# Expert rows transposed on the way in: DMA for TensorE and ScalarE, and one batch's normalization moved to VectorE

## The chip, the cores and the metric

The kernel runs on one core of a Trainium2 chip. The metric is the time of one execution on the device in microseconds. Seen in the profile are the core's engines: TensorE (matrix multiply, PE in the rows; PEld is its weight load), VectorE (DVE), ScalarE (ACT), GpSimd (POOL) and SyncE (SP), which only issues transfers. Each works through its own list of instructions in order; semaphores tie the lists together, and 16 DMA engines serve the transfers of all.

## What is computed

One gated block: cross-attention over a context of 77 tokens, added to x, then a layer of routed experts, added to that. x is 4 x 1024 x 256, float32. Cut to what matters:

```
x = x + tanh(g_xattn) * attention(layernorm(x), ctx)       # 4 batches x 1024 tokens, 77 keys each
h = layernorm(x)
gate = softmax(h @ gate_w + gate_b)                         # 8 experts
top_val, top_idx = top_k(gate, 2)
hidden = relu(h @ w1[e] + b1[e])                            # 256 -> 1024
expert_out[e] = hidden @ w2[e] + b2[e]                      # 1024 -> 256
x = x + tanh(g_ffn) * sum_k top_val[k] * expert_out[top_idx[k]]
```

Each token goes to two of eight experts. The kernel computes only the chosen ones.

## The kernel before

**Precision.** An expert's matmuls are done in float16 with each operand split into a high and a low half, so that three products stand for one of float32. The weights are split at the start: ScalarE writes the high part (hi_part, line 736), VectorE the low part (lo_part, line 958), for eight experts and two weights each. A token's normalized row is stored in the same way: high_rows on ScalarE (line 787) and low_rows on VectorE (line 1218) write 256 high and 256 low halves into xext, beside 8 gates and the token's number. That is a row of 265 words (XW), 1060 bytes.

**Routing.** For each batch of 1024 tokens VectorE picks the experts and a place for each token in a table in DRAM, xs, with 4096 rows for each expert. GpSimd writes the rows there with 16 indirect scatters a batch (scatter_rows, line 579). The table is then worked through in tiles of 128 rows that belong to one expert, S = 71 tiles. Of those, the tiles that are full after batch r may be read as soon as batch r is scattered; which table row a tile starts at, and which expert it is, lies in row_tab and exp_tab, made while the loop runs.

**The expert loop.** In iteration s of 71 each engine does its part, in an order written out by hand:
- SP, load_rows(s) (lines 487 to 501): reads the tile's first row from row_tab and loads 128 rows of xs into xg[s % 4], one transfer of 132.5 KB. Before it reuses the buffer it waits until tile s - 4 was transposed (line 497), its gates taken (line 498) and its indices copied (line 499).
- TensorE, turn_rows(s + 2) (line 1711): four 128x128 transposes of the row's high and low halves, into bank 5; then hidden(s + 1), 32 matmuls in eight column blocks (lines 1730 to 1734), and output(s), 24 matmuls (lines 1752 to 1754).
- ScalarE, rows_T(s + 2) (line 856): copies bank 5 to xTh[s % 2]; then h_bias (line 866), eight activations that add the bias to one half of the sums, h_hi (line 875), the high half of relu, and y_scale (line 882).
- VectorE: gate(s + 2) (line 1400), h_sum (line 1407), h_low (line 1415), y_sum (line 1422).
- GpSimd: index(s + 2) (line 652) and scatter(s) (line 660), an indirect transfer that adds 128 result rows to the output in DRAM. Scatter s waits until scatter s - 1 has landed.

**What runs beside it.** Attention for batches 0 and 1 and the splitting of the weights come before the loop. The attention of batches 2 and 3 runs inside it, one tile of 128 tokens for each iteration (attention_steps: iterations 2 to 16 and 18 to 32). A tile of attention goes through turn, rows_copy (line 767), scores (line 1593), score_in (line 1173) with the row maxima (line 1176), softmax_exp (line 772), turn_prob, attend and residual (line 1192). The parts attention_start, attention_mid and attention_end say where each engine does this between its expert work.

**Second normalization.** After attention a batch's 8 tiles of 128 tokens are normalized: rows_norm_2, on VectorE for batch 0 (line 1213) and on GpSimd for batches 1, 2 and 3 (line 612). It may start when the batch's x was stored to the output (s_outd). On GpSimd, batch 1 is done before the expert loop. ScalarE converts batch 1's rows (high_rows(1)) after its first two rows_T and ahead of the first h_bias.

**Buffers.** xg, xTh and the hidden buffers lie in pool0, in the space of the raw weights of two experts. The first transfers into it wait until VectorE is done with the first of these (s_lo1), hidden(0) until it is done with two (s_lo1 at 2), h_bias(0) for s_lo at 7 and VectorE's first h_sum for s_lo at 8.

Of the kernel before, what the change touches and what calls it, by code (L numbers as in the profile page):

```python
# [5 lines left out]
def gated_attention_and_routed_experts(  # L6
# [10 lines left out]
    ALU = mybir.AluOpType  # L17
# [35 lines left out]

    xs = nc.dram_tensor("xs", (E * N + P, XW), F32, kind="Internal").ap()

    with ExitStack() as ctx:
# [26 lines left out]

        xg = [carve(XW) for _ in range(U)]
        xTh = [carve(2 * ND * P, F16) for _ in range(2)]
        hb = carve(NH * P)
# [281 lines left out]
        g_ix = sem("g_ix")  # L368
        g_T = sem("g_T")
        g_xT = sem("g_xT")  # L370
        g_mm1 = sem("g_mm1")
# [9 lines left out]
        s_raw = [sem(f"s_raw{k}") for k in range(4)]  # L381
        g_xg = [sem(f"g_xg{u}") for u in range(U)]

        def tile_tokens(ap, b):
# [22 lines left out]
        ranked = bank[7][:, 2 * P:2 * P + 2 * E].rearrange("p (j e) -> p j e", j=2)  # L407
        turned_x = bank[5][:, 0:ND * P].bitcast(F16)
        summed = bank[4][:, 0:D]
# [20 lines left out]
        def _(sp):  # L430
# [58 lines left out]
            def load_rows(s):  # L489
                r = round_of(s)  # L490
                sp.wait_ge(s_tab, 3 * (r + 1))
                sp.wait_ge(s_scat, min(r + 1, B) * KO * T * 16)
                if r == B:
                    sp.wait_ge(s_pads, 2 * E * 16)
                    sp.wait_ge(s_zst, 16)
                if s >= U:
                    sp.wait_ge(g_T, s - U + 1)
                    sp.wait_ge(g_q, s - U + 1)
                    sp.wait_ge(g_ix, s - U + 1)
                row = sp.value_load(row_tab[0:1, s:s + 1], min_val=0, max_val=E * N)  # L500
                sp.dma_start(xg[s % U], xs[ds(row, P), :]).then_inc(g_xg[s % U], 16)

# [19 lines left out]
        def _(pool):  # L522
# [121 lines left out]
            root(3)  # L644
            rows_norm_2(1, 0, T)
            token_ids(1)

            def index(s):
                pool.wait_ge(g_xg[s % U], (s // U + 1) * 16)
                if s >= U:  # L650
                    pool.wait_ge(g_out, (s - U + 1) * 16)
                g.tensor_copy(idx[s % U][:], xg[s % U][:, TC:XW].bitcast(I32)).then_inc(g_ix, 1)

# [42 lines left out]
        def _(act):  # L696
# [134 lines left out]
            gate_exp(1)  # L831
            hi_part(7, 0)
            hi_part(6, 1)
            hi_part(7, 1)
# [10 lines left out]
            def attention_mid(s):  # L845
                for b, j in attention_steps(s):
                    for i in tile_at(j - 2):
                        rows_copy(b, i)
                    if j in (13, 14):
                        high_rows(b, 4 * (j - 13), 4 * (j - 12))  # L850

            def rows_T(s):
                act.wait_ge(g_T, s + 1)
                if s >= 2:
                    act.wait_ge(g_mm1, NHB * (s - 1))
                a.copy(xTh[s % 2], turned_x).then_inc(g_xT, 1)

# [25 lines left out]

            rows_T(0)
            rows_T(1)
            high_rows(1, 0, T)
            act.wait_ge(s_lo, E - 1)
# [3 lines left out]
            for s in range(S):  # L891
                attention_start(s)
                if s + 2 < S:
                    rows_T(s + 2)
                if s + 1 < S:
                    h_bias(s + 1)
                    h_hi(s + 1)
                attention_mid(s)
                y_scale(s)
# [3 lines left out]
        def _(dve):  # L903
# [426 lines left out]
            scales(3)  # L1330
            choose_2(1)
            lo_part(6, 0)
            gates(1)
# [62 lines left out]
            def gate(s, e):  # L1396
                if s >= U:
                    dve.wait_ge(g_y2, s - U + 1)
                dve.wait_ge(g_xg[s % U], (s // U + 1) * 16)
                v.tensor_tensor(q[s % U][:], xg[s % U][:, ds(e + GC, 1)].to_broadcast([P, 2]), inv[:, ds(2 * e, 2)], ALU.mult).then_inc(g_q, 1)  # L1400

# [45 lines left out]
        def _(pe):  # L1447
# [254 lines left out]

            def turn_rows(s):
                pe.wait_ge(g_xg[s % U], (s // U + 1) * 16)
                if s:
                    pe.wait_ge(g_xT, s)
                o = turned_x
                x16 = xg[s % U][:, 0:D].bitcast(F16)
                for c in range(ND):
                    for k in range(2):  # L1710
                        mm = t.transpose(o[:, (2 * c + k) * P:(2 * c + k + 1) * P],  # L1711
                                         x16[:, k * D + c * P:k * D + (c + 1) * P], ident16[:])
                mm.then_inc(g_T, 1)

            def hidden(s):
                pe.wait_ge(g_xT, s + 1)
                xt = xTh[s % 2]
                for c in range(NH):
# [43 lines left out]
            load_adr(0, 2 * NH)  # L1762
            turn_rows(0)
            turn_rows(1)
            pe.wait_ge(s_lo1, EB)
# [3 lines left out]
            for s in range(S):  # L1769
                if s == 1:  # L1770
                    pe.wait_ge(s_lo, E)
                if s + 2 < S:
                    turn_rows(s + 2)
                if s + 1 < S:
                    hidden(s + 1)
                else:
                    load_adr(s, 4 * NH)
                attention_mid(s)
                output(s)
                attention_end(s)  # L1780
# [28 lines left out]
```

## Time and profile before

| | us |
|---|---|
| median of 3 runs | 639.74 (639.56 to 641.3) |
| the profiled execution | 637.47 |
| its span in the profile | 635.7 |
| TensorE busy, matmuls (4723) | 521.8 (82%) |
| TensorE busy, weight loads (4724) | 432.8 (68%) |
| ScalarE busy (1061 instructions) | 416.6 (66%) |
| VectorE busy (1149) | 402.7 (63%) |
| GpSimd busy (296) | 286.0 (45%) |
| SP's queue (q1), share of the DMA engines | 18.7% |
| GpSimd's queue (q0) | 16.8% |

Busy is the time in which an engine has an instruction at work; matmuls overlap, and their ends are modelled. The profiled execution lies 2.3 us under the median, and 1.8 us of it are outside the span. The mean granted clock of TensorE is 0.875 of full speed. The span falls into three parts: up to about 144 us the weights, the attention of two batches and their routing; then the expert loop with attention inside it, to about 445 us; then the expert loop alone.

### The profile page before, as it was taken

The page shows a single profiled execution, that of the slowest core. Times are in us where ns is not written, and L with a number is a line of the kernel's source. Part 1 is how long each engine was busy: PE and PEld are TensorE (multiplying, and loading weights), DVE is VectorE, ACT ScalarE, POOL GpSimd, SP SyncE. Part 2 cuts the span into 40 slices and gives each one's busy share as a digit, 9 for nine tenths or more (in the row PEclk, how much of TensorE's full clock was granted, in tenths as well). Part 3 has the DMA queues.
Part 4 walks back from the last instruction along what each step waited for, and adds up shares of the span by engine and source line. Part 5 has one row for each costly group of instructions (what it writes and reads, how often), then busy time and mean ns, then how long its engine had stood idle before and what let it go on. Part 6 is the DMA issues. An engine that isn't in the chain of part 4 may idle for free.

```text
span 635.7 us, 15679 instructions
## 1 busy us (share of the span) xinstructions
PE 521.8 (82%) x4723; PEld 432.8 (68%) x4724; DVE 402.7 (63%) x1149; ACT 416.6 (66%) x1061; POOL 286.0 (45%) x296
## 2 busy tenths in 40 slices
PE   6958317506888999987799998879999999999991
PEld 3637216205567887765588887657999999999991
DVE  3268799487485667773467677745755566666650
ACT  2567874555456676664476675746888888888880
POOL 3110228574673323766532337666476632233331
PEclk8775555556899999998899999979999999999997
DMA  6919405723533223233232233233333333333221
GB/s 171 331 52 379 165 0 195 274 75 110 161 69 69 36 43 83 54 66 95 74 52 36 35 71 74 56 91 88 61 73 57 53 53 52 53 52 52 35 28 17
DMA packets 47633, 57.07 MB, mean 90 GB/s; under 512 B 6855, under 2 KB 43197, under 8 KB 47423
## 3 DMA queue, kind: packets, MB, share of 16 engines
q1 hardware_dynamic: 32223, 36.60, 18.7%
q0 software_dynamic: 14064, 18.55, 16.8%
q10 hardware_dynamic: 1264, 0.93, 0.5%
q8 instruction: 40, 0.66, 0.5%
q14 instruction: 42, 0.34, 0.2%
HBM read 33.19 MB, written 24.49 MB: 91 GB/s over the span
## 4 chain that ended last, share of the span: by engine, by line
PE 48%; DVE 16%; issue 10%; ACT 9%; DMA 6%; POOL 4%; SPq 2%; another core or an unknown queue 1%; ACTq 1%; DVEq 1%; POOLq 0%
PE hid L1730 8%; PE hid L1734 8%; PE bank L1752 6%; PE bank L1753 6%; PE bank L1754 6%; ACT pool L866 4%; PE hid L1731 4%; PE hid L1733 4%; POOL xb L612 3%; DMA out_dram<-pool,idx 3%; DVE pool L1407 2%; DMA xb<-in_x_dram 2%; DVE w1l L958 2%; PE bank L1711 2%; DVE w2l L958 2%
## 5 line engine op out<-in xcount | busy, mean ns | idle before, releaser
L660 POOL DMA_INDIRECT out_dram<-pool,idx x71 | 114.8, 1617 | 224.7 <-DVE pool L1422 190.4
L866 ACT ACTIVATE pool<-hid,b1s 128x128 f32<-128x128 f32 x568 | 167.7, 374 | 42.8 <-remote 24.1
L1730 PE MATMUL hid<-pool,w1h 128*128 128x256 f16 x568 | 159.1, 280 | 14.2 <-DVE pool L1407 7.5
L1752 PE MATMUL bank<-w2h,pool 128*128 x568 | 155.8, 274 | 9.5 <-issue 8.9
L1734 PE MATMUL hid<-pool,w1h 128*128 128x256 f16 x568 | 159.1, 280 | 1.9 <-issue 1.9
L1407 DVE TENSOR_TENSOR pool<-hid,pool 128x512 f32<-128x512 f32 x142 | 97.0, 690 | 96.3 <-ACT pool L866 96.2
L1753 PE MATMUL bank<-w2l,pool 128*128 x568 | 155.9, 274 | 2.1 <-issue 1.8
L1754 PE MATMUL bank<-w2h,pool 128*128 x568 | 155.9, 275 | 0.5 <-issue 0.5
L1731 PE MATMUL hid<-pool,w1l 128*128 128x128 f16 x568 | 127.2, 224 | 0.3 <-issue 0.3
L1733 PE MATMUL hid<-pool,w1l 128*128 128x128 f16 x568 | 127.1, 224 | 0.4 <-issue 0.3
L875 ACT ACTIVATE pool<-pool 128x512 f16<-128x512 f32 x142 | 90.1, 637 | 32.1 <-DVE pool L1407 31.6
L1415 DVE SCALAR_TENSOR_TENSOR pool<-pool 128x512 f16<-128x512 f32 x142 | 95.2, 686 | 5.4
L579 POOL DMA_INDIRECT xs<-xext,dest x64 | 72.8, 1137 | 31.0 <-issue 22.2
L1730 PEld LDWEIGHTS hid<-pool,w1h 128*128 x568 | 56.7, 100 | 24.0 <-issue 22.0
L1752 PEld LDWEIGHTS bank<-w2h,pool 128*128 128x128 f16 x568 | 55.9, 98 | 17.0 <-issue 9.9
L1753 PEld LDWEIGHTS bank<-w2l,pool 128*128 128x128 f16 x568 | 55.9, 98 | 12.0 <-issue 5.2
L1733 PEld LDWEIGHTS hid<-pool,w1l 128*128 x568 | 57.1, 100 | 8.7 <-issue 0.5
L1731 PEld LDWEIGHTS hid<-pool,w1l 128*128 x568 | 56.8, 100 | 7.5 <-issue 1.5
L1754 PEld LDWEIGHTS bank<-w2h,pool 128*128 128x128 f16 x568 | 55.9, 98 | 8.5 <-issue 1.7
L1734 PEld LDWEIGHTS hid<-pool,w1h 128*128 x568 | 56.9, 100 | 2.4 <-issue 2.4
L1422 DVE SCALAR_TENSOR_TENSOR pool<-pool,q 128x256 f32<-128x256 f32 x71 | 34.3, 484 | 32.7 <-ACT pool L882 26.1
L882 ACT ACTIVATE pool<-bank,q 128x256 f32<-128x256 f32 x71 | 33.5, 472 | 30.4 <-PE bank L1754 21.9
(257 smaller groups left out, 764.4 us busy)
## 6 DMA issues: line engine op xcount, KB each, us to landing
pool<-in_L_ffn_w_dram SPq DMA_DIRECT2D x12, 1024.0 KB
pool<-xs SPq DMA_DIRECT2D x71, 132.5 KB
xb<-in_x_dram SPq DMA_DIRECT2D x4, 1024.0 KB
out_dram<-xb SPq DMA_DIRECT2D x4, 1024.0 KB, 5.0
out_dram<-pool,idx POOLq DMA_INDIRECT x71
w1h<-in_L_ffn_w_dram SPq DMA_DIRECT2D x1, 1024.0 KB, 5.1
w1l<-in_L_ffn_w_dram SPq DMA_DIRECT2D x1, 1024.0 KB, 7.6
w2h<-in_L_ffn_w_dram SPq DMA_DIRECT2D x1, 1024.0 KB, 9.7
```

The costliest lines, as they stand in the source:

```text
L660: g.indirect_dma_start(out=out_rows, out_offset=bass.IndirectOffsetOnAxis(ap=idx[s % U][:, 0:1], axis=0), in_=y2[s % 3], in_offset=None, c ...
L866: a.activation(hb[:, c * P:(c + 1) * P], bank[c // 2][:, (2 * (c % 2) + 1) * P:2 * (c % 2 + 1) * P], ACT.Identity, bias=b1s[:, ds(e * NH + ...
L875: a.activation(hh[s % 2][:, half], hb[:, half], ACT.Relu).then_inc(g_hh, 1)
L1407: v.tensor_tensor(part, main, part, ALU.add).then_inc(g_hb, 1)
L1415: v.scalar_tensor_tensor(hl[s % 2][:, half], hb[:, half], 0.0, hh[s % 2][:, half], ALU.max, ALU.subtract).then_inc(g_hl, 1)
L1730: t.matmul(o, wh, xhl, start=True, stop=False)
L1731: t.matmul(o[:, 0:P], wl, xh, start=False, stop=False)
L1733: t.matmul(o[:, 0:P], wl, xh, start=False, stop=False)
L1734: mm = t.matmul(o, wh, xhl, start=False, stop=True)
L1752: t.matmul(o, hh[s % 2][:, hs], wh, start=c == 0, stop=False)
L1753: t.matmul(o, hh[s % 2][:, hs], wl, start=False, stop=False)
L1754: mm = t.matmul(o, hl[s % 2][:, hs], wh, start=False, stop=c == NH - 1)
```

## The change

An expert tile's rows no longer come as they lie. Of each tile SP issues four transfers with transpose=True, one for each 128x128 block of float16 (two column halves, high and low), from xs seen as float16 into xTh[s % 4], and then one transfer of the rest of the row, 9 words (8 gates and the token's number), into a smaller xg[s % 4]. TensorE's turn_rows, ScalarE's rows_T, bank 5's view and their semaphores are gone. There are now four xTh buffers instead of two, each with a semaphore g_xT[u], which hidden(s) waits for at 64 for each use. SP reuses the buffers of a slot when hidden(s - 4) is done (g_mm1), instead of when its rows were transposed; the waits for gates and indices stay.

The normalization of batch 1 after attention goes from GpSimd to VectorE, behind choose_2(1) and ahead of lo_part(6, 0). ScalarE's high_rows(1) moves from behind rows_T(1) to between hi_part(7, 0) and hi_part(6, 1). Batches 2 and 3 stay on GpSimd.

```
     xs = nc.dram_tensor("xs", (E * N + P, XW), F32, kind="Internal").ap()
+    xs16 = xs.bitcast(F16)
...
-        xg = [carve(XW) for _ in range(U)]
-        xTh = [carve(2 * ND * P, F16) for _ in range(2)]
+        xTh = [carve(2 * ND * P, F16) for _ in range(U)]
+        xg = [carve(XW - D) for _ in range(U)]
         hb = carve(NH * P)
...
         g_ix = sem("g_ix")
-        g_T = sem("g_T")
-        g_xT = sem("g_xT")
         g_mm1 = sem("g_mm1")
...
         g_xg = [sem(f"g_xg{u}") for u in range(U)]
+        g_xT = [sem(f"g_xT{u}") for u in range(U)]
...
         ranked = bank[7][:, 2 * P:2 * P + 2 * E].rearrange("p (j e) -> p j e", j=2)
-        turned_x = bank[5][:, 0:ND * P].bitcast(F16)
         summed = bank[4][:, 0:D]
...
                 if s >= U:
-                    sp.wait_ge(g_T, s - U + 1)
+                    sp.wait_ge(g_mm1, NHB * (s - U + 1))
                     sp.wait_ge(g_q, s - U + 1)
...
                 row = sp.value_load(row_tab[0:1, s:s + 1], min_val=0, max_val=E * N)
-                sp.dma_start(xg[s % U], xs[ds(row, P), :]).then_inc(g_xg[s % U], 16)
+                for c in range(ND):
+                    for k in range(2):
+                        sp.dma_start(xTh[s % U][:, (2 * c + k) * P:(2 * c + k + 1) * P],
+                                     xs16[ds(row, P), k * D + c * P:k * D + (c + 1) * P], transpose=True).then_inc(g_xT[s % U], 16)
+                sp.dma_start(xg[s % U], xs[ds(row, P), D:XW]).then_inc(g_xg[s % U], 16)
...
             root(3)
-            rows_norm_2(1, 0, T)
             token_ids(1)
...
                     pool.wait_ge(g_out, (s - U + 1) * 16)
-                g.tensor_copy(idx[s % U][:], xg[s % U][:, TC:XW].bitcast(I32)).then_inc(g_ix, 1)
+                g.tensor_copy(idx[s % U][:], xg[s % U][:, TC - D:XW - D].bitcast(I32)).then_inc(g_ix, 1)
...
             hi_part(7, 0)
+            high_rows(1, 0, T)
             hi_part(6, 1)
...
                         high_rows(b, 4 * (j - 13), 4 * (j - 12))
-
-            def rows_T(s):
-                act.wait_ge(g_T, s + 1)
-                if s >= 2:
-                    act.wait_ge(g_mm1, NHB * (s - 1))
-                a.copy(xTh[s % 2], turned_x).then_inc(g_xT, 1)
...
-            rows_T(0)
-            rows_T(1)
-            high_rows(1, 0, T)
             act.wait_ge(s_lo, E - 1)
...
                 attention_start(s)
-                if s + 2 < S:
-                    rows_T(s + 2)
                 if s + 1 < S:
...
             choose_2(1)
+            rows_norm_2(1, 0, T)
             lo_part(6, 0)
...
                 dve.wait_ge(g_xg[s % U], (s // U + 1) * 16)
-                v.tensor_tensor(q[s % U][:], xg[s % U][:, ds(e + GC, 1)].to_broadcast([P, 2]), inv[:, ds(2 * e, 2)], ALU.mult).then_inc(g_q, 1)
+                v.tensor_tensor(q[s % U][:], xg[s % U][:, ds(e + GC - D, 1)].to_broadcast([P, 2]), inv[:, ds(2 * e, 2)], ALU.mult).then_inc(g_q, 1)
...
-            def turn_rows(s):
-                pe.wait_ge(g_xg[s % U], (s // U + 1) * 16)
-                if s:
-                    pe.wait_ge(g_xT, s)
-                o = turned_x
-                x16 = xg[s % U][:, 0:D].bitcast(F16)
-                for c in range(ND):
-                    for k in range(2):
-                        mm = t.transpose(o[:, (2 * c + k) * P:(2 * c + k + 1) * P],
-                                         x16[:, k * D + c * P:k * D + (c + 1) * P], ident16[:])
-                mm.then_inc(g_T, 1)
-
             def hidden(s):
-                pe.wait_ge(g_xT, s + 1)
-                xt = xTh[s % 2]
+                pe.wait_ge(g_xT[s % U], (s // U + 1) * ND * 2 * 16)
+                xt = xTh[s % U]
                 for c in range(NH):
...
             load_adr(0, 2 * NH)
-            turn_rows(0)
-            turn_rows(1)
             pe.wait_ge(s_lo1, EB)
...
                     pe.wait_ge(s_lo, E)
-                if s + 2 < S:
-                    turn_rows(s + 2)
                 if s + 1 < S:
```

## Rows read from the trace of the kernel before

**Rows 1.** Stretches: busy us of PE, PEld, DVE, ACT, POOL; clock, DMA share.

```profile
322.00:376.00 54.00, 53.30 (x532) 46.79 (x530) 36.20 (x97) 38.14 (x119) 14.16 (x16) 1.00 0.25 37
...
505.00:600.00 95.00, 95.00 (x1041) 86.72 (x1040) 57.47 (x105) 79.64 (x209) 29.99 (x34) 1.00 0.31 50
```

**Rows 2.** Timeline, GpSimd: start us, us, engine, line; [idle before, releaser].

```profile
206.70 1.56 POOL L660 DMA_INDIRECT out_dram<-pool,idx  x1 [5.36 <-DVE pool L1422]
...
249.10 1.56 POOL L660 DMA_INDIRECT out_dram<-pool,idx  x1 [5.27 <-DVE pool L1422]
...
278.48 2.90 POOL L660 DMA_INDIRECT out_dram<-pool,idx  x1 [4.25 <-DVE pool L1422]
...
315.85 1.59 POOL L660 DMA_INDIRECT out_dram<-pool,idx  x1 [4.92 <-issue]
...
446.10 1.59 POOL L660 DMA_INDIRECT out_dram<-pool,idx  x1 [3.37 <-DVE pool L1422]
...
616.59 1.57 POOL L660 DMA_INDIRECT out_dram<-pool,idx  x1 [3.73 <-DVE pool L1422]
```

**Rows 3.** Chain that ended last, late stretch: start us, us, what.

```profile
603.71 0.22 PE bank L1711 x4
```

**Rows 4.** Timeline, ScalarE, one iteration with attention.

```profile
207.20 0.36 ACT L772 ACTIVATE pr<-pr,nms 128x77 f32<-128x77 f32 x1 [1.91 <-DVE nms L1176]
...
207.56 0.56 ACT L856 COPY pool<-bank 128x512 f16<-128x512 f16 x1
208.02 2.18 ACT L866 ACTIVATE pool<-hid,b1s 128x128 f32<-128x128 f32 x8
```

**Rows 5.** Timeline, TensorE's weight loads, the end of that iteration.

```profile
211.90 0.52 PEld L1593 LDWEIGHTS bank<-KQ,xT 128*128 128x128 f32 x4 [0.36 <-ACT xT L767]
```

**Rows 6.** Timeline at the loop's start: GpSimd, ScalarE, VectorE.

```profile
133.52 16.73 POOL L612 TENSOR_SCALAR xb<-xb,mv,rs 128x256 f32<-128x256 f32 x8 [0.69 <-DMA out_dram<-xb]
...
150.33 1.90 ACT L787 CAST xext<-xb 128x2048 f16<-128x2048 f32 x1 [4.60 <-POOL xb L612]
...
144.63 4.61 DVE L958 SCALAR_TENSOR_TENSOR w2l<-pool,scl,w2h 128x2048 f16<-128x2048 f32 x2
...
153.31 0.69 DVE L1407 TENSOR_TENSOR pool<-hid,pool 128x512 f32<-128x512 f32 x1 [1.96 <-ACT pool L866]
```

**Rows 7.** Groups by line: busy us, mean ns | idle before.

```profile
L1213 DVE TENSOR_SCALAR xb<-xb,mv,rs 128x256 f32<-128x256 f32 x8 | 2.7, 408 | 0.0
```

**Rows 8.** SP: timeline of first loads; line 501 in ns, min/median/max.

```profile
140.92 3.90 SPq L501 DMA_DIRECT2D pool<-xs  x4
...
L501 SPq DMA_DIRECT2D pool<-xs x71: 16/338/369, 140.9 to 591.7; - x71
```

**Rows 9.** Timeline, GpSimd, one indirect scatter of 128 rows.

```profile
119.48 0.96 POOL L579 DMA_INDIRECT xs<-xext,dest  x1 [0.30 <-issue]
```

**Rows 10.** Timeline, TensorE, the first transposes.

```profile
143.09 0.61 PE L1711 MATMUL bank<-ident,pool 128*128 128x128 f16 x4 [5.25 <-DMA pool<-xs]
```

**Rows 11.** SP's waits over the span: us in all, times, longest.

```profile
SPq L498 <- DVE q L1400: 152.7, 43, 11.4
```

**Rows 12.** DMA queues, 505 to 600 us: packets, MB, share of engines.

```profile
q0 software_dynamic: 2448, 2.23, 20.2%
q1 hardware_dynamic: 2436, 2.29, 9.5%
```

**Rows 13.** Timeline, GpSimd, four late scatters.

```profile
572.63 1.57 POOL L660 DMA_INDIRECT out_dram<-pool,idx  x1 [3.73 <-DVE pool L1422]
...
578.21 1.55 POOL L660 DMA_INDIRECT out_dram<-pool,idx  x1 [3.81 <-DMA out_dram<-pool,idx]
...
621.85 1.55 POOL L660 DMA_INDIRECT out_dram<-pool,idx  x1 [3.69 <-DVE pool L1422]
...
626.45 1.55 POOL L660 DMA_INDIRECT out_dram<-pool,idx  x1 [3.05 <-DMA out_dram<-pool,idx]
```

**Rows 14.** Waits from 281 to 316 us: us in all, times, longest.

```profile
ACT pool L866 <- remote: 10.0, 5, 3.7
```

## The prediction

> **What bounds the kernel now.** I began with the page, whose busy times put TensorE first, and then read stretches. From 505 to 600 us TensorE is busy all of the time at a granted clock of 1.00, its 2.4 GHz level, and the next engine, ScalarE, for 79.6 of 95 us; from 322 to 376 us TensorE is busy for 53.3 of 54 us [rows 1]. A busy engine need not set the pace, so the two stretches have to be told apart by their chains. GpSimd issues one accumulating scatter for each expert tile, and the starts of these scatters give the period of a tile [rows 2]. From 446.10 to 616.59 us there are 31 periods of 5.50 us. From 206.70 to 249.10 us, where the attention of the third batch (index 2 in the code) runs inside the expert loop, there are 6 of 7.07 us; the fourth batch repeats this with 6 more of 7.05 us.
>
> In the late stretch the chain of waits is TensorE alone, matmul after matmul without a gap, and the four transposes stand in it with 0.22 us [rows 3]. TensorE's own list of instructions is the bound there, and 0.22 us of 5.50 is what the change takes away.
>
> In the attention stretch the bound is a loop over three engines. ScalarE waits 1.91 us for VectorE's row maxima, runs the exponential, then the copy of the transposed rows (line 856) and the eight bias activations (line 866) without idle time between [rows 4]. VectorE's sums wait for these, ScalarE's line 875 for the sums, the copy of line 767 ends ScalarE's part, and TensorE, held 0.36 us for it [rows 5], scores the next attention tile, from which the maxima come. The row copy takes 0.56 us, but the first bias activation starts 0.46 us after it; those 0.46 us are inside the loop.
>
> **The change, part by part.**
>
> *Transposes and copy removed.* Four transposes and one copy go from each of 71 tiles. In the late stretch that is 31 x 0.22 = 6.8 us. In the 12 regular attention periods the loop loses 0.46 us: 5.5 us. TensorE doesn't stop this: of 7.05 us it has 0.36 idle and sheds at least the 0.22 of its transposes, so it could run at 6.47 against the loop's 6.59; it is then the next to be late. Of the 70 periods, 12 and 31 are now counted and the last two follow the last rows. Of the other 25, 11 lie where GpSimd puts four of a batch's row scatters between two accumulates, or right behind that; four of them, from 278.48 to 315.85, average 9.3 us [rows 2], and TensorE stands there for "issue" and for no row. I credit them nothing. Four are held by GpSimd's own normalization of the third and fourth batch, which stays: nothing. The remaining 10 get 0.3 us each, between 0.22 and 0.46: 3 us. Ends of this term: 0, and 25 x 0.46 = 11.5 us.
>
> *The second batch's normalization (index 1) on VectorE.* On GpSimd it took 16.73 us from 133.52 on; ScalarE waited 4.60 us for it before its conversion at 150.33, the first bias activations came behind that, and VectorE's first sum at 153.31 waited for them [rows 6]. On VectorE eight such rows took 2.7 us in the first batch [rows 7]. Their wait for the store of x1 costs nothing, since GpSimd's began at 133.52 and the place in VectorE's queue, behind choose_2(1), comes after that. Behind them are queued the low weight parts (line 958), the gates and the places, and SP, TensorE and ScalarE wait for the weight parts. The last pair, 4.61 us from 144.63, ends at 149.24 [rows 6], and so at 151.9. VectorE is then the one that is late: first sum at 151.9 for 153.31, a gain of 1.4 us. ScalarE's conversion (1.90 us) moves ahead of its last two weight parts, two engines' work side by side; VectorE, 2.7 us later itself, doesn't wait for them. TensorE's wait before its second tile shortens too, and it may keep the upper clock: I count nothing, at best 2 us.
>
> *Four transposing transfers and a short one.* No row shows a transposing transfer. SP needs 3.90 us for four loads now, of which the last instruction is 0.34: (3.90 - 0.34) / 3 = 1.19 us a load, 0.34 of it the transfer's own [rows 8]. Lower bound for a new tile: each of four more transfers like that instruction, 1.19 + 4 x 0.34 = 2.5 us of SP, and nothing below, since each is one more instruction. Upper bound: each like GpSimd's indirect scatter of 128 rows, 0.96 us with 0.30 of gap [rows 9], 1.19 + 4 x 1.26 = 6.2 us, on SP or in the queues. I take 0.5 us each, 3.2 us in all, near the lower end, because the transfers are issued by SP and with a direct pattern as the 0.34 us one is. That is hidden under a period of 5.28 us. The latency has more cover: a buffer comes free with hidden(s-4) and is read by hidden(s), four periods less a first layer of 2.6 us, so 18.5 us; a load now takes 2.2 us (issued at 140.92, used at 143.09 [rows 8, 10]). SP's last wait for a load is for VectorE's gates now (line 498, 152.7 us in all [rows 11]); the new one on g_mm1 comes about a first layer after it, and behind it stand only later loads and the stores of x1. The short transfer is last, so gates and indices get their data some 2 us later, inside the same cover. At the start there is none: SP is released by a weight part of VectorE, 2.7 us later than now, so it issues from 143.6; with 4 x 0.5 of issue and the rest of the landing hidden(0) starts at 147.3, while ScalarE may not begin its bias before 149.6, when the part that it waits for is done. At 1.26 each it is 150.0, and little of the 1.4 us is left.
>
> The DMA engines: from 505 to 600 us SP's queue takes 9.5% and GpSimd's 20.2% [rows 12], so 0.53 us of a tile for its 128 rows and 1.1 us for the accumulate. 512 pieces of 256 bytes and 128 short ones cost between once and five times the 0.53: 1.6 to 3.8 of 5.28 us with the accumulate.
>
> Of such a transfer only the notes have a price. The Trainium skill, "VectorE: DVE Perf Modes", section "The three transpose paths", gives 1309 ns for a 128x128 bf16 block by DMA and 390 ns on TensorE; this case's transposes take 0.22 us for four in a row, and no run here shows the other. An estimate from that page, if the transfers don't overlap, is 4 x 1.309 + 1.19 = 6.4 us a tile, which would be the first rival below. The Trainium skill, "Advanced Engine Details and Errata", section "X-Bar Transpose (TRN2)", says that such transfers are as fast as regular ones, which would be the forecast.
>
> **Sum.** 6.8 + 5.5 + 3 + 1.4 = 16.7 us. The profiled execution took 637.47 us (span 635.7); less 16.7 that is 620.8. The median of the runs shown stands 2.3 us above it, 639.74, so 623.0 us.
>
> **Rivals.**
>
> *1, slower: the transfers set the pace.* If a tile's five transfers take longer than 5.50 us on SP or in the queue, each late tile waits for its rows, and four buffers only put that off. At the upper bound the price is 31 x (6.2 - 5.50) = 21.7 us; attention's loop of 6.6 us stays the bound there (-5.5 us); the start and the ten other periods give nothing. 639.7 + 16.2 = 656 us. For it: five instructions in one queue instead of one. Against it: a load lands within 2.2 us. It decides from (5.50 - 1.19) / 4 = 1.08 us a transposing transfer on.
>
> *2, a smaller gain: the chain of accumulates.* A scatter waits for the landing of the one before. Undisturbed, the last two start 4.60 us apart [rows 13], which leaves 0.68 us under 5.28. One late scatter was held for its forerunner's landing and started 5.58 us after it, at 578.21 [rows 13]. If the denser queue does that to every tile, the late period is 5.58: 639.7 - 1.4 - 5.5 + 31 x 0.08 = 635 us.
>
> *3, slower: late issue.* From 281 to 316 us ScalarE's line 866 waits five times for something that the profile calls "remote", 10.0 us in all [rows 14], while the DMA queues are full of row scatters; the four periods there are 3.8 us longer than late ones. If the new transfers bring that about in every fourth late tile, it costs 8 x 3.8 = 30 us: 639.7 - 16.7 + 30 = 653 us.
>
> **How the numbers follow.** Forecast 623 us, chance 0.50; its own range is 612 (the other 25 periods at 11.5 us, the clock kept) to 631 (the other periods and the start at nothing, half of attention's gain). Rival 1 has 0.24, rival 2 0.10, rival 3 0.10, and 0.06 is for gains and losses that cancel. About 0.3% is what a measurement of this kernel can tell from no change. Faster by more: the forecast and most of rival 2, 0.58. Within it: 0.08. Slower: 0.34. The range of 611 to 660 holds the forecast and the three rivals at their prices and leaves out only dearer transfers than the upper bound.
>
> **What would show it.** Right: scatter starts 5.28 us apart late and 6.6 us in attention, line 1730 without idle time put down to the transfers into pool, the first sum near 152 us. Wrong: line 1730 waiting for those transfers from 446 us on (rival 1); line 660 waiting for its own landing in each tile (rival 2); more and longer waits for "issue" and "remote" in the late stretch (rival 3). If attention's period stays at 7.05, my reading of its loop is wrong; if the first sum is not before 153.3, VectorE's queue or the first landing was dearer than I took it. One transposing transfer of over 1.08 us in steady work would make the forecast wrong by itself.

## The result: 8% slower, and SP is the bound

| | before | after |
|---|---|---|
| median on the same chip, us | 639.65 (636.74 to 641.3, 4 runs) | 690.8 (687.99 to 697.78, 4 runs) |
| ratio, 95% interval | 1 | 1.0832 (1.0778 to 1.0885) |
| profiled execution, us (span) | 637.47 (635.7) | 691.21 (689.5) |
| mean granted clock | 0.875 | 0.854 |

The forecast was 623 us and the range ended at 660. The sign was wrong, and the mechanism that won is the first rival, at more than its price. The profile's page of the kernel after shows where to look. These are its busy times, the DMA packets and queues, and the shares of the chain that ended last, by engine and by line:

```profile
PE 526.9 (76%) x4439; PEld 420.4 (61%) x4440; DVE 396.8 (58%) x1157; ACT 381.8 (55%) x990; POOL 266.8 (39%) x288
...
DMA packets 93073, 57.08 MB, mean 83 GB/s; under 512 B 61383, under 2 KB 88637, under 8 KB 92863
...
q1 hardware_dynamic: 77663, 36.64, 21.5%
...
SPq 27%; PE 23%; DVE 14%; issue 14%; ACT 9%; DMA 8%; POOL 1%; another core or an unknown queue 1%; ACTq 1%; DVEq 1%; POOLq 0%
SPq L502 20%; PE hid L1711 5%; PE hid L1715 4%; ACT pool L863 3%; DVE pool L1400 3%; PE bank L1733 2%; PE hid L1712 2%; PE bank L1735 2%; PE hid L1714 2%; DMA xb<-in_x_dram 2%; PE bank L1734 2%; DMA out_dram<-pool,idx 2%; SPq L504 2%; DVE w1l L950 2%; SPq L499 2%
```

ScalarE and GpSimd have less to do, as the change says. No computing engine is full, and the queue of SP, which computes nothing, leads the chain with 27%, 20% of it the one line that issues the transposing transfers (502). SP's timeline at the loop's start is the plainest view (start, us, SP's queue, line, operation, count). A group x4 is one tile's four blocks:

```profile
138.15 5.03 SPq L502 DMA_TRANSPOSE pool<-xs  x4
143.40 0.41 SPq L504 DMA_DIRECT2D pool<-xs  x1
144.61 5.77 SPq L502 DMA_TRANSPOSE pool<-xs  x4
...
163.67 0.42 SPq L504 DMA_DIRECT2D pool<-xs  x1
164.14 0.42 SPq L510 DMA_DIRECT2D pool<-in_L_ffn_b_dram  x1
```

Then the line's own durations over the whole run (ns, min/median/max), and who waited for the short transfer (line 504), which is issued after the four:

```profile
L502 SPq DMA_TRANSPOSE pool<-xs x284: 21/1150/2510, 138.2 to 662.9; - x142
...
L504 SPq DMA_DIRECT2D pool<-xs x71: 212/427/1186, 143.4 to 664.2; - x71
...
  DVE q L1393: 81.3, 25
  POOL idx L654: 50.9, 19
```

A transposing transfer holds SP's queue for 1.15 us in the median, where a whole tile's plain load held it for 0.34 [rows 8]. The chain in the late stretch is SP, block after block. Its pieces in order of time are start, us, what:

```profile
599.17 1.14 SPq L502
...
600.44 1.15 SPq L502
...
603.12 0.42 SPq L504
...
604.45 1.14 SPq L502
...
608.26 2.18 SPq L502
...
610.65 2.56 DMA pool<-xs
...
613.44 0.16 DVE q L1393
```

One block starts 1.27 us after the other. Five instructions and their bookkeeping make a cycle of about 6.5 us, from 138.15 to 144.61 and here from 597.93 to 604.45, and now and then a block takes about a microsecond more, as the 2.18. That is above the 5.50 us that TensorE needed before [rows 2, 3]. In the kernel before, SP waited 152.7 us for VectorE's gates [rows 11]. In after no such wait is left, and SP's waits for a free buffer (line 497) come to 24.4 us in 10 times. SP is nearly always at work, and the others wait for it. A stretch that answers to [rows 1], its waits, and its scatter starts [rows 2]:

```profile
505.00:600.00 95.00, 82.86 (x797) 69.10 (x796) 44.59 (x86) 57.67 (x161) 33.00 (x37) 0.96 0.32 42
```

```profile
DVE q L1393 <- DMA pool<-xs: 72.6, 23, 5.1
```

```profile
470.83 1.58 POOL L662 DMA_INDIRECT out_dram<-pool,idx  x1 [4.74 <-DVE pool L1415]
...
529.14 1.56 POOL L662 DMA_INDIRECT out_dram<-pool,idx  x1 [2.86 <-DVE pool L1415]
...
670.99 1.57 POOL L662 DMA_INDIRECT out_dram<-pool,idx  x1 [3.90 <-DVE pool L1415]
```

TensorE was busy for 95.0 of 95 us and is now for 82.86. From 480 to 660 us VectorE's gates (line 1393) wait 72.6 us, 23 times, for rows. The 31 late periods take 200.2 us for 170.5: 6.46 us each, and 6.75 in the last 21, once the four buffers in hand are used up. (6.5 us is a cycle without a long block; about one transposing transfer in twelve takes a microsecond more.) The DMA engines aren't the bound: from 560 to 640 us their share by queue is

```profile
q0 software_dynamic: 1722, 1.57, 17.3%
q1 hardware_dynamic: 9230, 1.60, 13.4%
```

against 20.2% and 9.5% before [rows 12]. What is full is the list of instructions that issues, not what moves the bytes.

**Where the 53.8 us of the span come from**, by scatter starts. The loop's first accumulate starts 13.0 us later (177.95 for 164.99). The next four periods cost 2.2 us, the late stretch 29.7, and the stretches in which GpSimd's row scatters lie between the accumulates 4.1 (291.95 to 353.18 us in after) and 8.2 (423.38 to 470.83). The other periods with attention give back 2.8 and the last two 0.6: 13.0 + 2.2 + 29.7 + 4.1 + 8.2 - 2.8 - 0.6 = 53.8.

The change costs more at the start than these 13.0 us. VectorE finishes the variances of batch 1, which come ahead of anything that was changed, at 125.47 us in after and at 129.61 in before: the profiled execution of after happened to be 4.1 us quicker up to there (granted clock of the first 50 us 0.88 for 0.76). Counted from this mark, the first accumulate comes after 52.5 us instead of 35.4, which is 17.1 us later.

The start has a second cause beside the pace of SP. These are after's rows there, of VectorE and ScalarE (compare [rows 6]), and one wait from 138 to 200 us:

```profile
132.26 2.67 DVE L1205 TENSOR_SCALAR xb<-xb,mv,rs 128x256 f32<-128x256 f32 x8
...
152.49 0.16 DVE L1393 TENSOR_TENSOR q<-pool,inv 128x2 f32 x1 [4.71 <-DMA pool<-xs]
152.56 1.28 DVE L1400 TENSOR_TENSOR pool<-hid,pool 128x512 f32<-128x512 f32 x2
```

```profile
135.01 1.90 ACT L789 CAST xext<-xb 128x2048 f16<-128x2048 f32 x1
```

```profile
DVE xext L1210 <- DMA pool<-in_L_ffn_b_dram: 14.1, 1, 14.1
```

The normalization takes 2.67 us on VectorE and is over before its rows are wanted. VectorE's gate of the second tile, which stands ahead of its first sum, waits 4.71 us for that tile's short transfer, the tenth instruction of SP's list. And the bias of the second layer (line 510) is issued by SP behind four tiles' loads. These were four instructions and are now twenty, so it goes out at 164.14 (149.27 before), VectorE stands 14.1 us for it, and behind VectorE wait GpSimd's row scatters and its first accumulate.

### The profile page after: what moved, and what is told of

Same layout as the page of the kernel before. It is cut to its first block, busy times and chain, and to the rows that moved or that the text cites. A ratio compares the mean times of both kernels' runs of the same rounds, so it can differ in the third digit from the quotient of the medians.

```text
span 689.5 us, 15469 instructions
## 1 busy us (share of the span) xinstructions
PE 526.9 (76%) x4439; PEld 420.4 (61%) x4440; DVE 396.8 (58%) x1157; ACT 381.8 (55%) x990; POOL 266.8 (39%) x288
## 3 DMA queue, kind: packets, MB, share of 16 engines
q1 hardware_dynamic: 77663, 36.64, 21.5%
## 4 chain that ended last, share of the span: by engine, by line
SPq 27%; PE 23%; DVE 14%; issue 14%; ACT 9%; DMA 8%; POOL 1%; another core or an unknown queue 1%; ACTq 1%; DVEq 1%; POOLq 0%
SPq L502 20%; PE hid L1711 5%; PE hid L1715 4%; ACT pool L863 3%; DVE pool L1400 3%; PE bank L1733 2%; PE hid L1712 2%; PE bank L1735 2%; PE hid L1714 2%; DMA xb<-in_x_dram 2%; PE bank L1734 2%; DMA out_dram<-pool,idx 2%; SPq L504 2%; DVE w1l L950 2%; SPq L499 2%
## 5 line engine op out<-in xcount | busy, mean ns | idle before, releaser
L1711 PE MATMUL hid<-pool,w1h 128*128 128x256 f16 x568 | 164.9, 290 | 57.1 <-DVE pool L1400 37.0
L1715 PE MATMUL hid<-pool,w1h 128*128 128x256 f16 x568 | 165.4, 291 | 2.2 <-issue 2.2
L1733 PE MATMUL bank<-w2h,pool 128*128 x568 | 158.0, 278 | 11.1 <-issue 10.2
L1734 PE MATMUL bank<-w2l,pool 128*128 x568 | 157.9, 278 | 5.7 <-issue 5.7
L1735 PE MATMUL bank<-w2h,pool 128*128 x568 | 157.8, 278 | 5.3 <-issue 5.3
L1400 DVE TENSOR_TENSOR pool<-hid,pool 128x512 f32<-128x512 f32 x142 | 94.6, 687 | 86.1 <-ACT pool L863 80.1
L1712 PE MATMUL hid<-pool,w1l 128*128 128x128 f16 x568 | 131.1, 231 | 3.7 <-issue 3.6
L1714 PE MATMUL hid<-pool,w1l 128*128 128x128 f16 x568 | 131.1, 231 | 0.8 <-issue 0.8
L1711 PEld LDWEIGHTS hid<-pool,w1h 128*128 x568 | 58.6, 103 | 79.1 <-issue 76.8
L582 POOL DMA_INDIRECT xs<-xext,dest x64 | 70.6, 1103 | 35.4 <-issue 22.2
L1393 DVE TENSOR_TENSOR q<-pool,inv 128x2 f32 x71 | 12.0, 170 | 105.7 <-DMA pool<-xs 81.3
L1733 PEld LDWEIGHTS bank<-w2h,pool 128*128 128x128 f16 x568 | 56.7, 100 | 24.6 <-issue 16.2
L1712 PEld LDWEIGHTS hid<-pool,w1l 128*128 x568 | 58.7, 103 | 13.8 <-issue 3.5
L1714 PEld LDWEIGHTS hid<-pool,w1l 128*128 x568 | 59.1, 104 | 12.2 <-issue 1.7
L1715 PEld LDWEIGHTS hid<-pool,w1h 128*128 x568 | 59.2, 104 | 2.2 <-issue 2.2
L654 POOL COPY idx<-pool 128x1 int32<-128x1 int32 x71 | 38.3, 540 | 50.9 <-DMA pool<-xs 50.9
```

What stands on the lines that cost most here:

```text
L1400: v.tensor_tensor(part, main, part, ALU.add).then_inc(g_hb, 1)
L1711: t.matmul(o, wh, xhl, start=True, stop=False)
L1712: t.matmul(o[:, 0:P], wl, xh, start=False, stop=False)
L1714: t.matmul(o[:, 0:P], wl, xh, start=False, stop=False)
L1715: mm = t.matmul(o, wh, xhl, start=False, stop=True)
L1733: t.matmul(o, hh[s % 2][:, hs], wh, start=c == 0, stop=False)
```

## The experiments

The kernels ran on chips that differ in their absolute time (the kernel before took 611 to 640 us), so each is given as a ratio to the kernel before on the same chip. A ratio still moves a little from chip to chip: the same kernel gave 1.0832 and 1.0868 (after), and 0.9824 and 0.9737 (e9 and e14 below). So ratios of different chips that lie within 0.9% of each other say little. Theory 1 is that SP's time for each transposing instruction sets the pace, whatever the bytes. Its rivals: the bytes or the small pieces in the DMA queue, the landing of the last transfer of a tile, the order at the start, or VectorE's extra work.

**The change again, and its two halves apart.** The kernel after once more, beside those of the other groups; the normalization alone (e1); the transfers alone, with the normalization back on GpSimd (e7).

```
e1, on the kernel before:          e7, on the kernel after:
 root(3)                            root(3)
-rows_norm_2(1, 0, T)   # GpSimd   +rows_norm_2(1, 0, T)   # GpSimd
 ...                                ...
 choose_2(1)                        choose_2(1)
+rows_norm_2(1, 0, T)   # VectorE  -rows_norm_2(1, 0, T)   # VectorE
```

> The changed kernel again, unaltered, beside the next three on one chip. It gives the time that they are compared with and a second profile. SP's list paces the late stretch: late period 6.4 to 6.8 us, 1.27 us between transposing instructions, ratio to the kernel before 1.075 to 1.09.

> Only the normalization's move is made (VectorE normalizes batch 1, high_rows(1) goes ahead of the last weight parts); TensorE's transposes and ScalarE's copy stay. Theory 1 (GpSimd's 16.7 us held the loop's start by a little, VectorE's 2.7 us hold it by less): VectorE's first h_sum comes 1 to 2 us earlier measured from the variance of batch 1 (vv), late period 5.50 us unchanged, 637 to 639 us. Rival (the weight parts behind it are the bound, and the move costs its 2.7 us): 641 to 643 us.

> The changed kernel without its second part: batch 1 is normalized by GpSimd again and converted by ScalarE behind the last weight parts. Theory 1 (the four transposing transfers are all of the loss, the normalization's move is worth 1 to 2 us at most, and here nothing, since SP's first transfers decide): ratio to the kernel before 1.08 to 1.09, late period as in the changed kernel. Rival (the moved normalization delays the weight parts and with them SP's start): ratio 1.06 to 1.075.

Measured: after again 1.0868 (1.081 to 1.0926), e7 1.0805 (1.075 to 1.086), e1 0.9967 (0.994 to 0.9993): some 2 us faster. VectorE's extra work is harmless; the whole loss comes with the transfers. In after's second run the periods of 12 to 13 us of the row-scatter stretches are not there (7.2 to 7.8 us), and still the ratio is the same: from 439.75 to 649.70 us its 31 late periods take 6.77 us each. Beside the profile of e1, from another chip on which the kernel before takes 612 us, it loses 21.5 us up to the first accumulate and 41.9 in the late periods; all other stretches together give back 2.7.

**Plain transfers in place of transposing ones (e3).** The four blocks are copied as they lie. Nothing is transposed, so hidden layers are computed from wrong rows; the work of all engines is that of after.

```
-     xs16[ds(row, P), k * D + c * P:k * D + (c + 1) * P], transpose=True)
+     xs16[ds(row, P), k * D + c * P:k * D + (c + 1) * P])
```

> The changed kernel with its four transfers made plain (no transpose), same sizes, same places: the hidden layer gets rows that aren't transposed, so this leaves out the transposing itself. Theory 1 (only the transposing instruction is dear): 0.35 to 0.45 us an issue, SP at 3 to 3.4 us a tile, late period 5.28, 620 to 632 us; it is also what the removed transposes and copy are worth. Rival (it is the number of transfers and their small packets): late period over 6 us, 665 to 690 us.

Measured: 0.9899 (0.9848 to 0.9949). SP's first tile:

```profile
138.00 1.94 SPq L502 DMA_DIRECT2D pool<-xs  x4
140.13 0.33 SPq L504 DMA_DIRECT2D pool<-xs  x1
```

Five instructions of the same bytes in the same queue, at 0.53 us from one to the next, and the loss is gone; the regular late periods are 5.26 us. This is the cost at which the prediction had taken the transposing ones (0.5 us). The count of instructions alone is not the cause; the transposing one is.

**Wider blocks.** Two transposing transfers of 128x256 a tile (e2), then a single one of 128x512 (e6), for the same data:

```
e6:
-for c in range(ND):
-    for k in range(2):
-        sp.dma_start(xTh[s % U][:, (2*c+k)*P:(2*c+k+1)*P], xs16[ds(row, P), k*D+c*P:...], transpose=True)
+sp.dma_start(xTh[s % U].rearrange("p (j t) -> p j t", t=P), xs16[ds(row, P), 0:2 * D], transpose=True)
```

> The changed kernel with two transposing transfers of 128x256 a tile in place of four of 128x128, the same bytes. Theory 1 (SP is held about 1.27 us by each transposing instruction whatever its width, and SP's list paces the late stretch): SP needs 1.2 + 2 x 1.27 + 0.5 = 4.2 us a tile, the late period falls from 6.46 to TensorE's 5.3 us, the first scatter comes 10 us earlier, 630 to 645 us. Rival (the time goes with the transposed bytes, in the crossbar or the queues): 2.4 us an instruction, period 6.5 us, 685 to 692 us.

> The changed kernel with one transposing transfer of 128x512 a tile; the four blocks lie in xTh in another order and TensorE reads them with a stride. Theory 1 (SP is held 1.2 to 1.3 us by an instruction, whatever its width): SP needs 2.9 us a tile, late period 5.3, b2 is issued 10 us earlier than by two wide ones' 16 us, ratio to the kernel before 0.975 to 0.99. Rival (from some width on the time goes with the bytes): 2 to 4 us for the one instruction, SP 4 to 6 us, ratio 0.99 to 1.03.

Measured: e2 0.9965 (0.9936 to 0.9994), e6 0.9884 (0.9833 to 0.9935). SP's first tiles in e2, then in e6:

```profile
142.20 2.61 SPq L501 DMA_TRANSPOSE pool<-xs  x2
145.02 0.41 SPq L503 DMA_DIRECT2D pool<-xs  x1
146.24 3.06 SPq L501 DMA_TRANSPOSE pool<-xs  x2
```

```profile
138.19 1.33 SPq L500 DMA_TRANSPOSE pool<-xs  x1
...
140.97 1.22 SPq L500 DMA_TRANSPOSE pool<-xs  x1
```

A block four times as wide holds SP for the same 1.2 us. The time is a price of the instruction, not of its bytes. The bytes and their pattern are no bound here: e6 moves the same 36.6 MB on SP's queue, in 70,847 packets for after's 77,663. SP's cycle is 6.5 us with four, 4.0 to 4.5 with two and 2.8 with one. With two and with one TensorE is the bound again (in e6 it is busy for 59.57 of the 60 us from 500 us on), and the last periods are 5.26 us: the 0.22 us of the transposes are really won once SP keeps up. These two kernels are the change as it was meant, in a form that pays.

**Between the two: three transposing blocks and one plain (e12).** The fourth block is not transposed, so part of the result is wrong. The cycle should come out just above the 5.50 us from which the prediction said that the transfers decide.

```
-     ..., transpose=True)
+     ..., transpose=c + k < 2)
```

> The changed kernel with three transposing transfers a tile; the fourth block (low half of the second 128 columns) comes plain, not transposed, so the small correction that it holds is wrong. Theory 1 (SP's instructions add up): one instruction of 1.27 becomes one of 0.53 us, SP's cycle 6.46 becomes 5.7, late period 5.7 to 6.0 us, about 20 us less than the changed kernel, ratio to the kernel before 1.04 to 1.06. Rival (it is the transposes' landing, not SP, and three do no better than four): ratio 1.08.

Measured: 1.0468 (1.04 to 1.0537). SP's first two tiles:

```profile
137.70 3.75 SPq L502 DMA_TRANSPOSE pool<-xs  x3
141.66 0.42 SPq L502 DMA_DIRECT2D pool<-xs  x1
142.28 0.35 SPq L504 DMA_DIRECT2D pool<-xs  x1
143.44 4.20 SPq L502 DMA_TRANSPOSE pool<-xs  x3
```

A cycle of 5.74 us here, and 6.14 us a period from 472.72 to 613.97 us (23 of them; 5.97 over all 31 late ones), longer than the cycle by the blocks that take a microsecond more. The loss goes with the number of transposing instructions: four make 1.083 to 1.087, three 1.047, two 0.997.

**The order inside a tile (e5).** The short transfer with gates and indices goes ahead of the four.

> The changed kernel with the short transfer (gates and token number) ahead of the four transposing ones. Theory 1 (SP's instructions pace the late stretch, in whatever order; VectorE waits for the short transfer only since it is the last): VectorE's waits for it vanish and line hidden's waits for the transposed rows take their place, late period still 6.4 to 6.8 us, the ratio within 1% of the changed kernel's. Rival (the short transfer's late landing is itself the loss, for the gates are wanted two tiles ahead): late period near 5.3 us, 8% less time.

Measured: 1.0792 (1.0733 to 1.0852). Waits from 505 to 640 us:

```profile
DVE q L1393 <- DMA pool<-xs: 25.3, 19, 2.0
PEld hid L1711 <- DMA pool<-xs: 21.7, 19, 1.9
```

The gates no longer wait as long (75.2 us in after's second run, same stretch), and the matmuls wait for the blocks instead. A wait that changes its place while the period stays is the mark of a producer that is too slow: which transfer is last within the tile matters little (661.36 us for 666.02 on the same chip, 0.7%).

**The bias load earlier (e4, e8).** The load of line 510 goes behind the second tile's transfers instead of the fourth's, on the kernel after (e4) and on e6 (e8).

```
-for s in range(U):
+for s in range(2):
     load_rows(s)
 sp.wait_ge(s_lo, E)
 sp.dma_start(b2s, ...)
```

> The changed kernel with the load of b2 issued behind the second tile's transfers in place of the fourth's. Theory 1 (VectorE's wait of 14.1 us for b2 at the start is a loss of its own): b2 is issued near 151 us in place of 164, the first scatter comes 10 to 13 us earlier and 6 to 13 us of it stay to the end, 678 to 685 us. Rival (SP's list paces the kernel up to its end, so what is won at the start is waited for later): first scatter earlier, end unchanged, 689 to 692 us.

> As the one with a single transposing transfer of 128x512, and b2's load behind the second tile's transfers. Theory 1 (what is left of the loss at the start is the wait for b2): VectorE's wait for b2 goes to under 1 us and the first scatter comes 2 to 5 us earlier than without, ratio 0.97 to 0.985. Rival (the first tiles' rows are the later ones at the start): no change against the one without.

Measured: e4 1.0736 (1.0683 to 1.079), first accumulate at 166.18 us for 180.75 in after's second run; e8 0.9828 (0.9769 to 0.9886), 159.06 for 162.42 in e6. From the mark of batch 1's variances that is 11.5 us earlier in e4 and 3.0 in e8. So VectorE's wait for this load was real, and the lead isn't eaten later on: the last accumulate of e4 comes 14.7 us earlier than in after's second run, that of e8 4.0 us earlier than in e6. The medians say less for e4, about 1.3% of the time or 8 us (1.0868 and 1.0736, on two chips), between the two forecasts; after's second profile was the slowest execution of its four. For e8 and e6, on one chip, they say 4.1 us. Two periods of 13.65 and 12.83 us stand in e4 where after's second run has 8.0: at the first, GpSimd waits 6.49 us for the store of x before its normalization, and the accumulate waits behind it. Their neighbours are shorter, and the five periods around each cost only 1.0 and 1.9 us more.

**The expert's number (e9, e11, and the last pair).** In attention the period fell by 0.11 us instead of 0.46. ScalarE in after, one iteration:

```profile
235.95 0.36 ACT L774 ACTIVATE pr<-pr,nms 128x77 f32<-128x77 f32 x1 [2.01 <-DVE nms L1168]
236.22 0.19 ACT L774 ACTIVATION_READ_ACCUMULATOR pr<-pr,nms 128x1 f32 x1
236.67 2.17 ACT L863 ACTIVATE pool<-hid,b1s 128x128 f32<-128x128 f32 x8 [0.26 <-issue]
```

The exponential ends at 236.41, and ScalarE stands 0.26 us before the bias activations. In the chain of the kernel before ScalarE's queue reads the expert's number into a register at this place, beside the exponential:

```profile
207.29 0.28 ACTq L860
```

There the copy kept the engine at work until the biases began at 208.02, while the queue got on. The theory: with the copy gone, this reading is no longer covered. So it moves ahead of the exponential:

```
+if s + 1 < S:
+    bias_expert(s + 1)      # wait for the table, read the number
 attention_start(s)
 if s + 1 < S:
     h_bias(s + 1)
```

> The one with a single wide transfer and the early b2, and in it ScalarE reads the expert's number of the next tile (a register load) ahead of the attention's exponential in place of behind it. Theory 1 (in the attention stretch the removed copy of 0.46 us had this register load running under it, so that only 0.1 us was won, and the load now stands alone): ScalarE's idle 0.26 us before line h_bias goes, attention's period falls from 6.94 to 6.7 us, 12 periods, 2 to 4 us less, ratio to the kernel before 0.976 to 0.982. Rival (the loop has turned to TensorE's first layer): period 6.94 as before, ratio 0.983.

> The kernel before with the same register load moved ahead of the exponential. Theory 1 (there the load ran under the row copy and cost nothing): attention's period stays at 7.05 us (within 0.05). Rival (it is in the loop there too): 6.8 us.

> The kernel with one wide transfer and the early b2 again, as the base for the next on the same chip: ratio to the kernel before 0.978 to 0.988, attention's period 6.94, late period 5.3 us.

> That kernel with the expert's number read ahead of the exponential, on the same chip as its base. Theory 1 (attention's 12 regular periods and a few beside them each lose 0.3 us, and nothing gives it back): 3 to 5 us less than the base, 0.6% of the time. Rival (what attention wins is waited for later, at GpSimd's scatters): within 1 us of the base.

Measured: e9, on e8, 0.9824 (0.9773 to 0.9875) on a chip on which e8 hadn't run, a ratio that can't tell the two theories apart, though the attention period of 6.66 us can; e13, which is e8, 0.9817 (0.9773 to 0.986) and e14, which is e9, 0.9737 (0.9697 to 0.9777) on one chip, 600.23 and 596.54 us. e11, the same move in the kernel before, one run, 631.8 us for 634.49: its attention periods stay at 7.05. In e14:

```profile
226.53 0.36 ACT L772 ACTIVATE pr<-pr,nms 128x77 f32<-128x77 f32 x1 [1.84 <-DVE nms L1174]
226.79 0.19 ACT L772 ACTIVATION_READ_ACCUMULATOR pr<-pr,nms 128x1 f32 x1
226.88 2.15 ACT L866 ACTIVATE pool<-hid,b1s 128x128 f32<-128x128 f32 x8
```

The idle time is gone, and the regular periods are 6.65 us for 6.94: 12 x 0.29 = 3.5 us, close to the measured 3.7. In the kernel before the same move wins nothing in attention, since the copy covered it. The trace of after shows what was uncovered. The load itself (0.28 us) starts with the exponential and runs beside it; behind it the queue still has a register operation (0.15 us), a check of the value and the preparation of the first bias, and is through at 236.61, 0.2 us after the exponential's end. e14 is 2.6% faster than the kernel before and the best version of the study.

## Why the prediction was wrong, point by point

*Where the bound was.* Right for the late stretch: with SP out of the way (e2, e3, e6) the regular period is 5.26 to 5.30 us, which is 5.50 less 0.22. So the term of 6.8 us was sized rightly and is won, but only in those kernels.

*The transposing transfer at 0.5 us.* This is the step that failed. It measured 1.15 us on SP and 1.27 us from one to the next, so that a tile took 6.5 us of SP's list and not the 3.2 that were to be hidden under TensorE's 5.28. The prediction took a value near the lower bound "because the transfers are issued by SP and with a direct pattern as the 0.34 us one is". That is an argument from kinship, and e3 shows how far it goes: it holds for plain transfers of the same blocks (0.53 us) and says nothing on a transposing one. The upper bound (1.26 us) was within 1% of the truth, and the threshold of 1.08 us was right: e12's cycle of 5.7 us is slower than before, e2's of 4.0 to 4.5 isn't. With such a threshold between the bounds, and no row for the operation, 0.50 for the forecast and 0.24 for the rival was too bold. Of two statements on such transfers in the Trainium skill, one would have given the right answer. The estimate of 6.4 us a tile, from the Trainium skill's "VectorE: DVE Perf Modes", section "The three transpose paths", is what SP's cycle came to (6.5 us). The section's 1309 ns stand there for a block, though, and here the like time is one of the instruction. The Trainium skill's "Advanced Engine Details and Errata", section "X-Bar Transpose (TRN2)", says that such transfers are as fast as regular ones. For SP's time that doesn't hold: 1.27 us for 0.53.

*Rival 1's price, 656 us.* The mechanism was right, the sum short by 35 us (in the profiles, 53.8 us for its 16.2). Late it had 31 x 0.7 = 21.7 us where 29.7 came, as the cycle is 6.5 us and not 6.2, and blocks of 2 to 2.5 us come on top. Attention gave back 2.8 us, not 5.5. The start was put at nothing and lost 13.0 us and another 2.2 in the next four periods. The row-scatter stretches were put at nothing too and cost 12.3.

*The start.* The normalization's gain came, in part by luck. In e1, which has it alone, the first sum comes 22.4 us behind the mark of batch 1's variances, for 23.7 in before: 1.3 us, where 1.4 were forecast. But the last pair of weight parts ends 0.7 us later by that mark, not 2.7, and VectorE then stands 1.76 us before its gates. It lost less than its 2.7 us because its own instructions run shorter when GpSimd doesn't normalize beside them (the product of gates and mask takes 0.22 us in after and e1, 0.45 in before and e7). In after the first sum at 152.56 looks like the forecast 151.9, but only because that execution was ahead by 4.1 us; by the mark it is 3.4 us later than in before. One step was not carried through: SP's transposing transfers were costed for hidden(0), not for the gate of the second tile, nor for the bias load that stands behind four tiles, nor for VectorE, GpSimd and the first accumulate behind that.

*Attention, 12 x 0.46 us.* The loop was read rightly, but the copy was taken out as if nothing lay beneath it. 0.11 us came; 0.26 of the rest was ScalarE's idle time behind the reading of the expert's number, which the copy had covered. With that moved the period is 6.65 for the forecast 6.59 (e14).

*The accumulates (rival 2)* hardly showed in after (one wait of 0.9 us from 480 to 660 us). In e14, where the tiles come fast enough, GpSimd does wait for its own landing late (31.2 us in 9 waits, from 480 to 560 us), but the regular period holds at 5.26.

*Late issue (rival 3).* Not in the late stretch. In the row-scatter stretches after's first profile has more of it: ScalarE's biases wait 18.0 us for "remote" from 276 to 330 us (10.0 before, [rows 14]), and those stretches cost 12.3 us in all. After's second run, on another chip, has no such wait and the same ratio, so the verdict doesn't hang on it. The long periods go with the chip: every profile from where the kernel before takes 634 us or more has them (before, after, e7, e9, e11), and none from the other chips, where the same periods are 7.1 to 8.1 us. Where they are, the four narrow transfers make them longer still (12.3 us at the first of them in after and 12.2 in e7, 9.8 in before, e9 and e11). What makes them stays open.

## What to carry to other kernels

Price an issuing queue like an engine: count its instructions for a tile, measure one of each kind, and compare the sum with the period, because a transfer that moves few bytes can hold its queue longer than the work that it replaces takes (4 x 1.27 us on SP for 0.22 us of TensorE and 0.46 of ScalarE). Where the price is one of the instruction and not of its bytes, make the instruction wide before giving up the idea. When an operation is removed, list what ran under it in the same engine's queue and what stands behind its replacement in the other queue; both come to light only when the cover is gone.

## What the runs showed of the hardware

A transposing transfer from DRAM holds SP for about 1.2 us whether it is 128x128, 128x256 or 128x512 float16 (medians 1.15, 1.19 and 1.22 us); a plain one of 128x128 holds it for 0.33. Of the transposing ones 21 of 284 in after, 13 of 142 in e2 and 6 of 71 in e6 took 1.6 to 2.5 us; no run explains why single ones take so much longer. A number read into a register just behind an exponential of 0.46 us, where nothing else is at work, leaves ScalarE idle for 0.26 us before the instruction that needs it. VectorE's product of 64 elements a partition took 0.45 us while GpSimd normalized and 0.22 when it didn't.
